# A four-layer conditioned stack on one core: ten of twelve modulation blocks are moved from the lead-in into the first three attention slots

## The reference, cut to what matters

```python
# layer 0: LayerNorm, modulated, 16 query heads of 32 on 4 key heads, a sparse mask
proj = t_emb @ W_ada.T + b_ada;  scale, shift = proj[:, :C], proj[:, C:]
h = (x - mu) * rsqrt(var + eps) * (1 + scale) + shift
q = h @ Wq.T;  c_kv = h @ Wkd.T;  k = c_kv @ Wku.T;  v = c_kv @ Wvu.T
x = x + softmax(rope(q) @ rope(k).T / sqrt(32), masked) @ v @ Wo.T
# layer 1: RMS norm scaled by ln_w * (1 + t @ tw.T), 8 heads of 64 on one key head, gated MLP of 2048
# layer 2: ada = silu(cond) @ Wada.T + bada (6 x 512), cosine attention of 16 heads, gelu MLP
# layer 3: 8 experts, eo = silu(emb) @ emb_W + emb_b (2 x 512) modulates a LayerNorm, output projection
```

## Time and profile before

| | |
|---|---|
| three runs | 2404.94, 2404.7, 2399.85 us |
| profiled execution | 2398.59 us, its span 2396.8 us |
| PE (TensorE) busy | 2244.7 us, 94% of the span |
| VectorE (DVE), ScalarE (ACT), POOL busy | 1168.9, 1033.6, 292.5 us |
| first score of layer 0 | 93.49 us after the start |

### The profile page before, as it was taken

How to read it: one execution, slowest core, us unless ns; L and a number is a source line. 1 busy time by engine, 2 the same in 40 slices (tenths; PEclk the granted TensorE clock), 3 DMA queues, 4 the chain that set the end, 5 groups by cost and what they waited for, 6 DMA issues and landing times.

```text
span 2396.8 us, 34593 instructions
## 1 busy us (share of the span) xinstructions
PE 2244.7 (94%) x14034; PEld 1511.1 (63%) x14034; DVE 1168.9 (49%) x2499; ACT 1033.6 (43%) x2425; POOL 292.5 (12%) x246
## 2 busy tenths in 40 slices
PE   5889999999999999999999989999999989999998
PEld 2455555555555687888877756565664668888633
DVE  2345454454457344433443356657587554544322
ACT  2355555444446221111113366657676552222473
POOL 3331122122021001110001010101010110000021
PEclk9889999999999999999999999999999999999999
DMA  8310020000010002110102211011110101100001
GB/s 274 113 40 27 15 64 26 23 23 18 18 40 27 31 27 84 54 61 27 36 6 79 79 53 67 31 63 36 54 36 19 53 1 36 36 1 1 1 18 53
DMA packets 59487, 104.97 MB, mean 44 GB/s; under 512 B 10592, under 2 KB 24560, under 8 KB 59328
## 3 DMA queue, kind: packets, MB, share of 16 engines
q1 hardware_dynamic: 58368, 100.30, 12.6%
q0 software_dynamic: 960, 2.45, 0.3%
HBM read 77.04 MB, written 10.49 MB: 37 GB/s over the span
## 4 chain that ended last, share of the span: by engine, by line
PE 84%; ACT 7%; DVE 6%; POOL 1%; issue 1%; SPq 1%; DMA 1%; DVEq 0%; POOLq 0%; ACTq 0%
PE banks L1213 36%; PE banks L404 22%; PE banks L740 6%; PE banks L732 4%; PE banks L756 4%; ACT sb_Pr L842 2%; PE banks L766 2%; PE banks L265 1%; ACT sb_PT L847 1%; PE banks L906 1%; DVE sb_hN L364 1%; PE banks L630 1%; PE banks L638 1%; DVE sb_Pr L812 1%; PE banks L890 1%
## 5 line engine op out<-in xcount | busy, mean ns | idle before, releaser
L1213 PE MATMUL banks<-sb_HH,sb_Ws 128*128 128x512 f32 x1536 | 490.2, 392 | 12.7 <-DVE sb_HL L1103 7.3
L1213 PEld LDWEIGHTS banks<-sb_HH,sb_Ws 128*128 128x128 f32 x1536 | 289.6, 189 | 76.7 <-issue 16.7
L1213 PE MATMUL banks<-sb_hidH,sb_Ws 128*128 128x512 f32 x1024 | 331.2, 392 | 0.4 <-DVE sb_x L1284 0.4
L842 ACT ACTIVATE sb_Pr<-sb_Pr,sb_nmax 128x512 f32<-128x512 f32 (+4 forms) x512 | 291.6, 576 | 30.9 <-DVE sb_nmax L812 30.8
L1213 PE MATMUL banks<-sb_HL,sb_Ws 128*128 128x512 f32 x768 | 300.0, 391 | 0.0
L847 ACT ACTIVATE sb_PT<-banks 128x512 f32<-128x512 f32 (+2 forms) x320 | 143.5, 496 | 302.6 <-PE banks L740 225.5
L740 PEld LDWEIGHTS banks<-sb_ident,sb_Pr 128*128 128x128 f32 x1536 | 169.7, 142 | 125.5 <-issue 38.9
L819 DVE COPY sb_PT<-banks 128x512 f32<-128x512 f32 (+2 forms) x320 | 168.6, 563 | 163.1 <-PE banks L740 108.7
L740 PE MATMUL banks<-sb_ident,sb_Pr 128*128 128x128 f32 x1536 | 214.2, 282 | 18.2 <-DVE sb_A L830 5.0
L1213 PEld LDWEIGHTS banks<-sb_hidH,sb_Ws 128*128 128x128 f32 x1024 | 192.3, 188 | 44.0 <-issue 2.5
L1213 PE MATMUL banks<-sb_hidL,sb_Ws 128*128 128x512 f32 x512 | 199.4, 389 | 0.0
(11 more groups left out here) (160 smaller groups left out, 3251.7 us busy)
## 6 DMA issues: line engine op xcount, KB each, us to landing
sb_ring<-split_units SPq DMA_DIRECT2D x48, 512.0 KB, 3.3
sb_ropet<-sb_R SPq DMA_DIRECT2D x70, 128.0 KB, 2.0
sb_staged<-in_L_cond_Wfc SPq DMA_DIRECT2D x16, 512.0 KB, 4.6
sb_wada<-in_L_cond_Wada SPq DMA_DIRECT2D x6, 1024.0 KB, 5.5
split_units<-sb_unitpair SPq DMA_DIRECT2D x12, 512.0 KB, 2.9
sb_x<-in_x SPq DMA_DIRECT2D x4, 1024.0 KB, 9.1
sb_staged<-in_L_cond_Wg SPq DMA_DIRECT2D x8, 512.0 KB, 3.7
sb_staged<-in_L_cond_Wu SPq DMA_DIRECT2D x8, 512.0 KB, 4.7
```

The costliest lines, as they stand in the source:

```text
L842: ins = e.activation(prob, prob if s.biased else k.bank(n % 4)[:, 0:s.width(u)], ACT.Exp, bias=s.stat(k, k.nmax, b, u), scale=-1.0 if s.bi ...
L1213: mm = e.matmul(bank, lhsT, rhs, start=i == 0, stop=i == len(mats) - 1)
```

## The change

The lead-in (all that comes before the first score) keeps modulation blocks 0 and 1. The other ten go into the sides of the attention slots of layer 0: blocks 2, 3, 4 into slot 0, 5 to 8 into slot 1, 9 to 11 into slot 2, mixed evenly into the first part of each slot's sides (the norm of batch 1 and the projections in slot 0, the projections in slots 1 and 2). These ten share one buffer: the load of block n waits for the products of block n-1. In slot 0 the rotary beats and the next norm's beats now follow each other, where they were mixed. In the lead-in the order of beats is written out, the key group 6 of `proj0` goes before the second tile of q, and DVE's reduction of the angles comes after the norm. On SP's queue x of batch 0 is the first load, the projection weights and the tables come from SP and not POOL, x of batches 2 and 3 and the output weights follow the key rows of batch 0, and the block loads follow the key rows and swaps of each batch. The key rows of each tile have a semaphore of their own, and the scores of tile c wait for that one. The buffers of the block weights, `ada_rows`, `cond` and `sel` lie elsewhere.

```diff
@@ the lead-in
-        start = pre(0, 0, 1, 2)
         blocks = [ada.block(0), ada.block(1) + ada.turn(0), ada.turn(1)] + \
             [ada.block(j) + (ada.turn(j - 1) if j > 2 else []) for j in range(2, BLOCKS)] + [ada.turn(BLOCKS - 1)]
-        lead = [(ada, 0, "act", "silu", 0), (angles, 0, "dve", "reduce", 0), (angles, 0, "act", "sin", 0),
-                (angles, 0, "act", "cos", 0), (angles, 0, "dve", "negate", 0)] + start[0] + sum(blocks[:3], []) + \
-            fold(start[1:], (0, len(start) - 1, blocks[3:])) + [(ada, 0, "act", "scales", 0)] + \
-            [(ada, 0, "dve", "comb", i) for i in range(len(combs))]
+        n0, p0, r0 = pre(0, 0), pre(0, 1), pre(0, 2)
+        turned = [(angles, 0, "act", "sin", 0), (angles, 0, "act", "cos", 0), (angles, 0, "dve", "negate", 0)]
+        lead = [(ada, 0, "act", "silu", 0)] + \
+            sum([n0[0], blocks[0], n0[2], blocks[1], n0[3], blocks[2], n0[5], n0[6], [(angles, 0, "dve", "reduce", 0)],
+                 p0[0], p0[1], p0[6], p0[2], r0[0], turned, p0[3], r0[1], p0[4], r0[2], p0[5], r0[3], p0[7], r0[4]], [])
+        combined = lambda *which: [[(ada, 0, "dve", "comb", i) for i in which]]
+        later_blocks = [blocks[3:6] + [ada.turn(4)] + combined(0, 1), [ada.block(5)] + blocks[7:10] + [ada.turn(8)] + combined(2, 3),
+                        [ada.block(9)] + blocks[11:13] + [ada.turn(11)] + combined(4, 5, 6) + [[(ada, 0, "act", "scales", 0)]]]
         sides01 = []
         for m in range(2 * B - 1):
             late = beats(posts[m - 1]) if m else []
-            sides01.append(([] if m else pre(1, 0)) + pre(m + 1, 1) + among(late, pre(m + 1, 2), pre(m + 2, 0)) + [[]])
+            if m < 3:
+                first = (pre(1, 0) if m == 0 else []) + pre(m + 1, 1)
+                rest = pre(1, 2) + pre(2, 0) if m == 0 else among(late, pre(m + 1, 2), pre(m + 2, 0))
+                sides01.append(among(first, later_blocks[m]) + rest + [[]])
+            else:
+                sides01.append(pre(m + 1, 1) + among(late, pre(m + 1, 2), pre(m + 2, 0)) + [[]])
@@ scores of layer 0
-            if u == 0:
-                e.wait_ge(*s.k_loaded(b))
+            if u % (s.U // C) == 0:
+                e.wait_ge(*s.k_loaded(b, c))
...
-                       near=lambda b, i, h: VN[:, b % 2, i - 1, 32 * h:32 * h + 32], k_loaded=lambda b: (l_k, 16 * 15 * (b + 1)), turned_fresh=[("ada", 0, "turn", BLOCKS - 1)])
+                       near=lambda b, i, h: VN[:, b % 2, i - 1, 32 * h:32 * h + 32], k_loaded=lambda b, c: (l_k[c], 16 * (4 if c < C - 1 else 3) * (b + 1)))
@@ buffers
-        wada = [place(f"wada{i}", 30464 + 2048 * i, [P, C, D]) for i in range(3)]
-        ada_rows = place("ada_rows", 36608, [P, 2, D])
+        wada = [place(f"wada{i}", o, [P, C, D]) for i, o in enumerate((17408, 19456, 6144))]
+        ada_rows = place("ada_rows", 4864, [P, 2, D])
+        wada_of = lambda j: min(j, 2)
@@ SP's queue, lead-in
-            for n, (name, j) in enumerate(blocks):
-                if n >= 3:
-                    done("ada", 0, "block", n - 3)
-                e.dma_start(wada[n % 3][:], rows(name)[:, :, j * D:(j + 1) * D]).then_inc(l_ada[n % 3], 16)
-                for b in {0: (0,), 4: (1,), 8: (2, 3)}.get(n, ()):
-                    e.dma_start(x[:, :, b, :], xrows[:, :, b, :]).then_inc(l_x[b], 16)
...
+            load_x(0)
+            load_block(0)
+            load_block(1)
+            for dst, name in ((wkd, "L0_cond_Wkd"), (wq0, "L0_cond_Wq")):
+                e.dma_start(dst, rows(name)).then_inc(l_w[0], 16)
+            for dst, name in ((wku, "L0_cond_Wku"), (wvu, "L0_cond_Wvu")):
+                e.dma_start(dst, a[name]).then_inc(l_w[0], 16)
+            for dst, name in ((perm, "perm"), (k.cosr, "cos0"), (k.sinr, "sin0")):
+                e.dma_start(dst[:], a[name]).then_inc(l_rope, 16)
+            e.dma_start(mask0[:], a["mask0"].rearrange("(i p) t -> p i t", p=P)).then_inc(l_bias[0], 16)
+            load_x(1)
+            load_block(2)
...
@@ SP's queue, batch by batch
                 for c in range(C):
-                    if c == C - 1:
-                        e.wait_ge(l_k, 16 * (15 * b + 12))
+                    for before in range(C - 1) if c == C - 1 else ():
+                        e.wait_ge(l_k[before], 64 * (b + 1))
                     for strip in range(4 if c < C - 1 else 3):
                         e.dma_start(k.R[32 * strip:32 * strip + 32, b % 2, 1, c, :], heads[32 * c:32 * c + 32, :])\
-                            .then_inc(l_k, 16)
+                            .then_inc(l_k[c], 16)
                 for g in range(2, 5) if b else ():
                     swap(rope0, b, g)
+                if b == 0:
+                    load_x(2)
+                    load_x(3)
+                    e.dma_start(wo0, rows("L0_cond_Wo")).then_inc(l_wo0, 16)
+                for n in ((3, 4, 5), (6, 7, 8, 9), (10, 11), ())[b]:
+                    done("ada", 0, "block", n - 1)
+                    load_block(n)
+                if b == 2:
+                    done("ada", 0, "turn", len(blocks) - 1)
+                    for dst, name in ((wk1, "L1_cond_Wk"), (wv1, "L1_cond_Wv"), (wo1, "L1_cond_Wo")):
+                        e.dma_start(dst, rows(name)).then_inc(l_w[1], 16)
```

More of the change, by code:

```diff
@@ L105, with __init__ @@
     name = "ada"
-    def __init__(s, cond, w, loaded, rows, sel, mod, modb, plus, combs, first_loaded, cols_loaded, cond_loaded):
+    def __init__(s, cond, w, loaded, rows, sel, mod, modb, plus, combs, first_loaded, modb_loaded, cols_loaded,
+                 cond_loaded):
         s.cond, s.w, s.loaded, s.rows, s.sel, s.mod, s.modb = cond, w, loaded, rows, sel, mod, modb
         s.plus, s.combs = plus, combs
-        s.first_loaded, s.cols_loaded, s.cond_loaded = first_loaded, cols_loaded, cond_loaded
+        s.first_loaded, s.modb_loaded, s.cols_loaded, s.cond_loaded = first_loaded, modb_loaded, cols_loaded, cond_loaded
     def block(s, j):
@@ L1401, in conditioned_stack @@
         l_first, l_rope, l_cols, l_cond = sem("l_first"), sem("l_rope"), sem("l_cols"), sem("l_cond")
-        l_ada = [sem(f"l_ada{i}") for i in range(3)]
+        l_ada, l_modb = [sem(f"l_ada{i}") for i in range(3)], sem("l_modb")
         k.s_angle, l_wo0 = sem("s_angle"), sem("l_wo0")
@@ L1410, in conditioned_stack @@
         l_wq1 = sem("l_wq1")
-        l_k = sem("l_k")
+        l_k = [sem(f"l_k{c}") for c in range(C)]
         k.l_swap = [sem(f"l_swap{i}") for i in range(2)]
@@ L1465, in conditioned_stack @@
         BLOCKS = ADA * P // D
-        ada = Ada(cond, lambda j: wada[j % 3], lambda j: (l_ada[j % 3], 16 * (j // 3 + 1)), ada_rows, sel[:], mod, modb,
-                  [float(j in (0, 2, 3, 6, 7, 10)) for j in range(BLOCKS)], combs, (l_first, 16 * 6),
+        wada_of = lambda j: min(j, 2)
+        ada = Ada(cond, lambda j: wada[wada_of(j)], lambda j: (l_ada[wada_of(j)], 16 * max(j - 1, 1)), ada_rows, sel[:],
+                  mod, modb,
+                  [float(j in (0, 2, 3, 6, 7, 10)) for j in range(BLOCKS)], combs, (l_first, 16 * 3), (l_modb, 16 * 3),
                   (l_cols, 16 * n_cols), (l_cond, 16))
@@ L1513, in keys @@
                     return (mlp_up("mlp1", ended[0]), mlp_down("mlp1", LAST))[b]
-                return scores_end(*p) if p else []
+                return scores_end(*p) if p else [("ada", 0, "block", 1)] if b else []
             return keys
@@ L1848, in _, with load_x @@
             xrows = a["x"].rearrange("(c p) b t -> p c b t", p=P)
-            for n, (name, j) in enumerate(blocks):
-                if n >= 3:
-                    done("ada", 0, "block", n - 3)
-                e.dma_start(wada[n % 3][:], rows(name)[:, :, j * D:(j + 1) * D]).then_inc(l_ada[n % 3], 16)
-                for b in {0: (0,), 4: (1,), 8: (2, 3)}.get(n, ()):
-                    e.dma_start(x[:, :, b, :], xrows[:, :, b, :]).then_inc(l_x[b], 16)
[L1855 to L1864, removed]
+            def load_x(b):
+                e.dma_start(x[:, :, b, :], xrows[:, :, b, :]).then_inc(l_x[b], 16)
@@ new lines, in load_block @@
+            def load_block(n):
+                name, j = blocks[n]
+                e.dma_start(wada[wada_of(n)][:], rows(name)[:, :, j * D:(j + 1) * D]).then_inc(l_ada[wada_of(n)], 16)
+            load_x(0)
[5 more added lines that the diff above has]
+                e.dma_start(dst, a[name]).then_inc(l_w[0], 16)
@@ new lines, in _ @@
+            for dst, name in ((perm, "perm"), (k.cosr, "cos0"), (k.sinr, "sin0")):
[3 more added lines that the diff above has]
+            load_block(2)
+            for name, _ in COLS:
+                e.dma_start(col[name], a[name]).then_inc(l_cols, 16)
+            e.dma_start(k.smul[:], a["L2_cond_scale_mul_log"]).then_inc(l_cols, 16)
+            e.dma_start(k.strip[:], a["strip"]).then_inc(l_cols, 16)
@@ L1985, in _ @@
             for name, t0, n in MODB:
[L1986 to L1989, removed]
-            e.dma_start(wvu, a["L0_cond_Wvu"]).then_inc(l_w[0], 16)
```

(7 more changed lines are left out.)

13 lines of the change are left out of this document (5 added, 8 removed).

## The result

Medians of the runs taken together: 2402.7 us before, 2411.1 us after (13 runs each), a ratio of 1.0031 with a 95% interval of 1.0021 to 1.0041. The kernel became **slower by 0.3%**; 2395 us was forecast. The profiled executions are 2398.6 and 2412.4 us, 13.8 apart. Of this 8.6 us lie in the front, up to layer 1's first score (439.4 us before, 448.0 after). The other 5 us lie behind it, where both kernels issue the same instructions. They are spread between executions: in the fourteen profiled executions of this document that part takes 1956.7 to 1962.5 us, and the kernel after happens to have the longest (1957.4 before). What is left, 8.6 us, is what the medians show (8.4).

A forecast was written before the change was run, and what follows sets the result against it. PE was taken to bound the kernel, holding 84% of the chain. The terms -38.5 + 14.8 + 10.9 + 7.3 gave -5.5 us, 2393.1 from 2398.6; with 2 us added the forecast was 2395 us, its own range 2388 to 2401.

The forecast's parts named there:

- The lead-in: Everything before the first score: first score at 55 us against 93.49, so -38.5 us, between -43 and -33.
- The price of the moved work: Blocks and turns in slots 0 to 2: 1.0 us each on PE, plus 0.9 us per bank wait.
- Slot 1: Four blocks and four turns 8.0 us, three bank waits 2.7, some gaps filled: +10.9 us, bounds 5 and 18.
- Slot 0: Blocks 2 to 4, their turns and the unmixed order: 4.2 + 5.3 - 2.5 + 7.8 = +14.8 us (7 to 22).
- Start to first projection: Slot 0's start: block 3's load holds the variance, projection 23.4 us in, +4.2 us, bounds 0 and 8.
- Projections: Slot 0's projections: blocks and turns 3.0 us, bank wait 0.7, 2.6 more points at 0.6: +5.3 on 32.2.
- To PE's resumption: Slot 0's rotary part after the projections: 18.5 instead of 21.0 us, as the norm's sum no longer delays POOL; -2.5.
- Slots 2 and 3: Slot 2: 6.0 + 1.8 - 0.5 = +7.3 us, bounds 3 and 13; slot 3, using layer 1's weights: nothing.
- C: Rival, slots: loads through the single buffer put 24 us on PE, 2414 us; chance 0.18.
- A: Rival, slots: PE's gaps swallow the moved work, 12 us more absorbed, 2383 us; chance 0.26.
- B: Rival: no measurable change, lead-in gains 35 us or slot 0 loses 18; 2399 to 2405 us; chance 0.22.
- D: Rival, scores: the wait per key tile works but is worth nothing; within the forecast, no chance of its own.

The follow-up runs named there:

- turnfirst: The changed kernel with the turn of block j-1 ahead of block j and not behind it; 2402.2 us, 0.9996 of before.
- noada: The changed kernel with blocks 2 to 11, their turns and their loads left out; 2376.6 us, 0.9884 of before.
- noload: The changed kernel without the loads of blocks 3 to 11, which multiply with block 2's weights; 2413.6 us, 1.0045 of before.
- mixed0: The changed kernel with slot 0's rotary and next-norm beats mixed again as before the change; 2404.6 us, 1.0003 of before.
- b_swap2: The kernel before with a semaphore per key tile and swaps 2, 3, 4 issued behind the copies of tiles 0, 1, 2; 2393.0 us, 0.9956 of before.
- b_keywait: The kernel before with only the wait per key tile, a semaphore for each tile; 2401.2 us, 0.9993 of before.

## Why the prediction failed, step by step

The front came out 8.6 us longer, where -5.5 was the sum: 14.1 us apart. Of these 7.6 lie in slot 0, 3.7 in slot 1, 0.9 in slot 2 and 1.9 in slot 3.

- **The lead-in: right.** -38.5 forecast, -38.4 measured, with x, variance, projection and score each within 1.5 us. Part of this is luck in the terms. The 3 us a megabyte for a queue that does nothing else stand in no row of before, and the trace after has block 0 land 4.8 us behind x (12.5 and 7.7). And of where the gain comes from, the prediction counts nine blocks and nine turns, 18 us, but ten of each leave the lead-in.
- **The price of the moved work: the step that failed.** The prediction put it as "1.0 us each", plus 0.9 us for a wait of the bank. The products take 1.06 us only at the high clock; in slot 0 they took 1.9. And the waits for ACT's copy cost more than their length: 5.3 us of them in seven places, of which turnfirst took away 3.4, with 8.4 us of the time. noada puts the whole at 31.1 us in the front, where the forecast's terms for them come to 25.2 at most (20.0 for the products, 0.7, 2.7 and 1.8 for the bank). Slot 1 is the clearest: +10.9 forecast, +14.6 measured, 12.7 of it PE's own busy time.
- **Slot 0: two terms too small.** +14.8 forecast, +22.4 measured. Start to first projection +8.8 and not +4.2: I had let block 3's load hold it, behind which blocks 2 and 3 and turn 2 cost nothing. noload shows that the load holds nothing, and noada that these products cost 4.9 us on top of a chain that starts 3.9 us later. Projections +6.3 and not +5.3. To PE's resumption -3.2 and not -2.5. Behind it +10.5 and not +7.8 (26.6 against 16.1 us). In noada, without blocks, this part is 12.9 us longer than before (29.1), so the unmixed order does this and not the moved work; mixed0, with the order of before, takes 7.4 us off the slot. The clock is low there, 0.59, but it was 0.63 in this part before. The mechanism, DVE waiting 12 us for a swap behind 15 copies, was right (11.8), and b_swap2 shows on the kernel before that the order on SP makes this wait.
- **Slots 2 and 3.** +8.2 against +7.3; and 1.9 us in slot 3 that I had put at nothing.
- **The rivals.** C, the single buffer, has nearly the time measured and is not the cause: noload took its waits away and gained nothing. A, that the gaps swallow the moved work, is refuted by noada: the work costs 31 us for 20 us of products, so the gaps gave next to nothing. B's amount for slot 0 (18 us more) was passed, but its lead-in held. D, the wait per key tile worth nothing, is shown by b_keywait on the kernel before.

What the prediction weighed and left out of its sum was the clock. I let slot 0's longer wait give back the slot's warm start and charged nothing for the low clock that short waits bring in slots 1 and 2. The Trainium skill's page TensorE: Matmul & The Clock Gate, HAM oscillation, says that waits for transfers drop PE to the low clock. Behind DVE's 11.8 us wait for a swap, in which PE stood still for 10.9 us, the trace agrees (0.59 over the rest of the slot). That section's case does not cover slot 1: there the clock fell with no wait for a transfer and none over 0.72 us, and there the measurement decides.

Left open: what the low clock alone costs, since no run changes it without also changing waits; the 8.9 us above are an estimate.

## What to carry to other kernels

Work moved from a stage with idle time into one where the engine is full costs its duration there, plus the wait at each hand-over through a shared bank, plus what those waits do to PE's clock; price it from rows of the stage that it goes to. Where two steps share one bank, put the one whose input has long been ready first: reversing two items of a list gave back this loss. Order a queue by who waits next, not by kind: on the kernel before, six small swaps issued between key copies were worth some 9 us, and an earlier start without this (b_keywait) was worth nothing. And where two edits don't add, look at the clock as well as at the idle time.

## What the runs showed of the hardware

In slot 1 of the kernel after, PE's clock went to its lower level (0.50 of full speed, 1.2 GHz) between 185 and 190 us, after 5 us in which PE was busy for 3.8 us and waited 0.72 us at most at a time. In turnfirst the waits at that place were 0.47 and 0.27 us instead of 0.47 and 0.72, and the same products and the projection behind them ran at the high level (3.7 us and not 4.9). Executions of one kernel differ with the clock: the thirteen of the kernel after went from 2406.3 us at a mean of 0.974 to 2414.1 us at 0.971.

And an issue on SP is not always cheap. At the head of the kernel after, two issues took 3.0 and 3.5 us while megabyte loads stood in the queue; the four issues behind them (10.95 to 13.44 us) took 0.55 to 0.63 us each:

```profile
4.37 3.02 SPq L1872 DMA_DIRECT2D sb_W<-in_L_cond_Wq  x1
7.44 3.47 SPq L1874 DMA_DIRECT2D sb_W<-in_L_cond_Wku  x1
```
